# Top-k attention stage of a two-layer vision tower: when router weights and queries are loaded, and where the follow-up parts stand

## The reference

```python
# layer 1 attention: causal, but each query keeps only its 32 largest scores
scores = jnp.einsum('bhqd,bhkd->bhqk', q, k) / math.sqrt(D_HEAD)
scores = jnp.where(causal, neg_inf, scores)
vals, idx = jax.lax.top_k(scores, K_S)                  # K_S = 32
masked = jnp.put_along_axis(jnp.full_like(scores, -jnp.inf), idx, vals, axis=-1, inplace=False)
y = (softmax(masked) @ v) @ Wo.T + bo
h = h + y
# layer 1 router: a two-layer SELU network of 256 -> 1024 -> 256, and the two largest of its 256 outputs
gate_logits = selu(layernorm(h) @ gate_wi + gate_bi) @ gate_wo + gate_bo
topv, topi = jax.lax.top_k(gate_logits, 2)
```

## Time and profile before

| | |
|---|---|
| median of 3 runs | 2192.14 us (2188.59 to 2197.21) |
| the profiled execution's own time | 2191.06 us |
| its span | 2189.4 us |
| busy share of the span | DVE 67%, PE 66%, PEld 40%, ACT 38%, POOL 27% |
| `attend_top`, from its first DVE instruction to `weight` | 1198.0 to 2147.9 us |

### The profile page before, as it was taken

One profiled execution on the slowest core, in us unless ns is written; L12 is line 12 of the kernel. 1 busy time (PEld: TensorE's weight loads), 2 busy tenths in 40 slices (PEclk: granted clock), 3 DMA queues, 4 the chain that ended last, 5 costly groups with the idle time before them and its releaser, 6 DMA issues. The chain is left out here.

```text
span 2189.4 us, 35237 instructions
## 1 busy us (share of the span) xinstructions
PE 1453.4 (66%) x10364; PEld 865.4 (40%) x10397; DVE 1469.3 (67%) x4767; ACT 825.5 (38%) x2043; POOL 592.2 (27%) x1044
## 2 busy tenths in 40 slices
PE   6489888948887608999346266576656666666651
PEld 3122225524443504666223144454445444444440
DVE  4578876747775611111245499989997999799905
ACT  2256663215554202222013244355435443544320
POOL 4100001210000060000343144455435544554341
PEclk9699998969999758999758556567656665766675
DMA  5572220443331321111217400110021002100001
GB/s 162 162 261 66 77 66 8 137 133 78 77 77 70 169 77 36 46 43 44 68 49 207 111 1 1 40 40 1 1 47 32 2 1 50 30 2 1 1 1 39
DMA packets 87485, 137.61 MB, mean 63 GB/s; under 512 B 9720, under 2 KB 68000, under 8 KB 85540
## 3 DMA queue, kind: packets, MB, share of 16 engines
q1 hardware_dynamic: 84068, 127.38, 20.0%
q0 software_dynamic: 3264, 8.41, 1.2%
HBM read 82.50 MB, written 53.76 MB: 62 GB/s over the span
## 5 line engine op out<-in xcount | busy, mean ns | idle before, releaser
L1359 DVE MATCH_REPLACE8 top_left<-top_next,top_left 128x65 f32<-128x65 f32 (+15 forms) x768 | 322.2, 427 | 0.0
L1354 DVE MAX8 top_next<-top_left 128x8 f32<-128x65 f32 (+15 forms) x768 | 300.7, 432 | 0.0
L1255 POOL TENSOR_TENSOR top_e<-top_e,top_left 128x129 f32<-128x129 f32 (+15 forms) x256 | 191.3, 769 | 243.5 <-DVE top_left L1359 243.5
L1125 ACT ACTIVATE top_e<-top_ps_s,top_neg_max 128x129 f32<-128x129 f32 (+15 forms) x256 | 126.0, 492 | 344.3 <-POOL top_neg_max L1240 339.9
L1003 PE MATMUL top_ps_pt<-ident,top_e 128*128 128x128 f32 x640 | 149.7, 364 | 130.3 <-POOL top_e L1255 85.3
L686 DVE TENSOR_REDUCE tok_rowmax<-tok_ps_s 128x1 f32<-128x512 f32 x256 | 167.0, 688 | 42.4 <-PE tok_ps_s L528 39.7
L1901 DVE TENSOR_TENSOR moe_hid<-moe_act_gate,moe_ps_h 128x512 f32<-128x512 f32 x39 | 26.8, 688 | 220.0 <-ACT moe_act_gate L1862 220.0
L1003 PEld LDWEIGHTS top_ps_pt<-ident,top_e 128*128 128x128 f32 x640 | 106.1, 189 | 153.5 <-issue 149.0
L686 DVE TENSOR_REDUCE rot_rowmax<-rot_ps_s 128x1 f32<-128x128 f32 (+3 forms) x256 | 115.7, 488 | 47.1 <-PE rot_ps_s L531 43.1
L659 ACT ACTIVATE tok_et<-tok_ps_st 128x1024 f32<-128x1024 f32 x128 | 124.2, 1021 | 51.6 <-PE tok_ps_st L562 51.6
L1801 PE MATMUL moe_ps_h<-moe_w,moe_rows_t 128*128 x312 | 142.3, 599 | 0.2 <-issue 0.2
(11 more groups left out here) (332 smaller groups left out, 3118.0 us busy)
## 6 DMA issues: line engine op xcount, KB each, us to landing
moe_w<-in_moe_w SPq DMA_DIRECT2D x3, 4096.0 KB, 24.0
moe_xs<-zeros SPq DMA_DIRECT2D x1, 5120.0 KB, 20.6
last_xs<-zeros SPq DMA_DIRECT2D x1, 5120.0 KB, 33.6
moe_rows<-moe_xs SPq DMA_DIRECT2D x40, 128.0 KB
moe_ys<-moe_y SPq DMA_DIRECT2D x38, 128.0 KB, 1.7
v_rows<-tok_va SPq DMA_DIRECT2D x4, 1024.0 KB
tok_vs<-v_rows SPq DMA_DIRECT2D x16, 256.0 KB
v_rows<-rot_va SPq DMA_DIRECT2D x4, 1024.0 KB
```

Of the source, the lines that this page charges most:

```text
L1125: act.activation(e[:, U % KEPT, 0:keys(U)], row(U), ACT.Exp, bias=neg_max[:, U % 4:U % 4 + 1]).then_inc(e_ok, 1)
L1255: pool.tensor_tensor(e[:, U % KEPT, 0:w], e[:, U % KEPT, 0:w], left[:, U % 4, 0:w], ALU.subtract).then_inc(prob_ok, 1)
L1354: dve.max(next8[:, U % 2, step // 2, :], left[:, U % 4, 0:keys(U)]).then_inc(pick, 1)
L1359: ins = dve.match_replace(left[:, U % 4, 0:w], next8[:, U % 2, step // 2 - 1, :], left[:, U % 4, 0:w], 0.0)
```

## The change

- The six weight tensors get their buffers ahead of `norm` (`upper_weights`), and SP issues their DMAs in `norm`, right behind the three of `top_w`, `top_qkb` and `top_vb`. They count on one semaphore, `c.upper_in`. `gate_bi` is negated by POOL at the start of `attend_top`; the wait and the instruction on DVE are gone.
- From the second image on a group's queries and keys wait for the last scores of the group in the image before (`s_mm`), no longer for its last product; the values still wait for that product. The values of group g are issued behind the queries and keys of group g+1, in the first image too.
- Follow-up parts are placed by half rounds. `follow(k, 0)` stands ahead of the round's work on PE and ACT, and in mid-round on DVE, right behind `largest`; `follow(k, 1)` stands at the end. On POOL both stand at the end. A planner walks over the half rounds with an estimated start of each, 0.8 + 0.0083 x keys us for each unit, and an estimated duration of each part, and places the parts of the normed run (`denominators` to `normed_out`) and the routed run (`hidden` to `search`) of neighbouring steps where they fit. It also keeps who used `ps_x` last, and `bank_free` waits for that.
- The two buffers of `summed`, `x_t`, `hid` and `logits` become one each.
- In the last step T=16 `scale`, `add_residual`, the final line of `normalise`, both `join` and `add_bias` run on DVE (the square root stays on POOL), and the second half of `hidden` writes a bank of the scores, so that it need not wait for the first.

The diff, cut to what is spoken of:

```diff
-        def step_at(k, lag):
-            T, rest = divmod(k - START - lag, 8)
-            return T if rest == 0 and 0 <= T < STEPS else None
+        NORMED = (("denominators", DVE, 0.5), ("scale", POOL, 1.5), ("turn_context", PE, 2.0), ("context_out", ACTE, 1.0),
+                  ("project_out", PE, 4.0), ("sum_copy", ACTE, 1.0), ("residual", POOL, 2.0), ("moments", DVE, 1.0),
+                  ("normalise", POOL, 3.0), ("turn_normed", PE, 2.0), ("normed_out", ACTE, 1.0))
+        ROUTED = (("hidden_0", PE, 4.0), ("hidden_out_0", ACTE, 3.0), ("hidden_1", PE, 4.0), ("join_0", POOL, 0.0),
+                  ("hidden_out_1", ACTE, 3.0), ("join_1", POOL, 3.0), ("route", PE, 8.0), ("logits_out", ACTE, 1.0),
+                  ("add_bias", POOL, 1.0), ("search", DVE, 1.0))
+        begins, at = [], 0.0
+        for k in range(rounds):
+            own = sum(0.8 + 0.0083 * keys(U) for U in (2 * k, 2 * k + 1))
+            begins += [at, at + own / 2]
+            at += own
...
+        while routed_run[0] < STEPS:
+            for run, parts in ((routed_run, ROUTED), (normed_run, NORMED)):
+                ahead_of = -1
+                while run[0] < STEPS:
+                    T, i, free = run
+                    name, engine, us = parts[i]
+                    if free > (begins[half] if ahead_of < 0 else begins[half + 1] - us) or engine <= ahead_of:
+                        break
+                    if name in TO_BANK and in_bank:
+                        break
...
+                    step_of[name, half] = T
...
+                    ahead_of = engine if engine != DVE else 9
+                    run[:] = (T, i + 1) if i + 1 < len(parts) else (T + 1, 0), max(free, begins[half]) + us
...
         @block.sync
         def _(sp):
             for b in range(B):
-                for g in range(G):
-                    if b:
-                        sp.wait_ge(pv_mm, G * (NQ * b - 1) + g + 1)
-                    load_step(sp, c, b, g, qs[g], ks[g], loaded[g])
-                    load_by_position(sp, c, b, g, vs[g], v_loaded[g])
-                if b == 0:
-                    sp.dma_start(wo[:, :, :], a["top_wo"]).then_inc(w_in, 16)
...
+                for g in range(G + 1):
+                    if g < G:
+                        if b:
+                            sp.wait_ge(s_mm, PER_TILE * (NQ * b - 1) + 4 * g + 4)
+                        load_step(sp, c, b, g, qs[g], ks[g], loaded[g])
+                    if g:
+                        if b:
+                            sp.wait_ge(pv_mm, G * (NQ * b - 1) + g)
+                        load_by_position(sp, c, b, g - 1, vs[g - 1], v_loaded[g - 1])
...
@@ VectorE
                     if 2 * k + 3 < units:
                         largest(2 * k + 2)
                         largest(2 * k + 3)
+                follow(k, 0)
+                if k < rounds:
                     for step in (2, 4):
...
                     for u in pair:
                         take(u, 6)
-                follow(k)
-                if k == START:
-                    dve.wait_ge(w_in, 16 * 6)
-                    dve.tensor_scalar(less_bi[:, :], gate_bi[:, :], -1.0, None, ALU.mult).then_inc(ready, 1)
+                follow(k, 1)
...
-def norm(c, tag, fetch):
+def norm(c, tag, fetch, ahead):
...
             c.fetch(sp, fetch)
+            for dst, src in ahead:
+                sp.dma_start(dst, src).then_inc(c.upper_in, 16)
```

More of the change, by code:

```diff
@@ L810, in attend_top @@
     KEPT = 8
-    START = 2
     STEPS = NT + 1
+    LAST = STEPS - 1
+    READY = 3
+    PE, ACTE, POOL, DVE = range(4)
+    UPPER = 16 * 6
+    wo, bo = w_out
+    gate_wi, gate_bi, gate_wo, gate_bo = gate
     HC = HIDDEN // P
@@ new lines, in attend_top @@
+        ROUTED = (("hidden_0", PE, 4.0), ("hidden_out_0", ACTE, 3.0), ("hidden_1", PE, 4.0), ("join_0", POOL, 0.0),
+                  ("hidden_out_1", ACTE, 3.0), ("join_1", POOL, 3.0), ("route", PE, 8.0), ("logits_out", ACTE, 1.0),
+                  ("add_bias", POOL, 1.0), ("search", DVE, 1.0))
+        TO_BANK = ("turn_context", "project_out", "turn_normed", "hidden_0", "hidden_1", "route")
+        FROM_BANK = ("context_out", "sum_copy", "normed_out", "hidden_out_0", "hidden_out_1", "logits_out")
@@ new lines, in attend_top, with bank_free @@
+        LAST_ROUND = half // 2 + 1
+        def bank_free(eng, name, T):
+            if bank_before[name, T] is not None:
+                part, t = bank_before[name, T]
+                sem, count = {"context_out": (ct_out, t + 1), "sum_copy": (sum_out, t + 1),
+                              "normed_out": (x_out, t + 1), "hidden_out_0": (relu_ok, 2 * t + 1),
+                              "hidden_out_1": (relu_ok, 2 * t + 2), "logits_out": (l_out, t + 1)}[part]
+                eng.wait_ge(sem, count)
@@ L943, in tile, with due @@
+        def due(name, k, half):
+            return step_of.get((name, 2 * k + half))
         def tile(T):
@@ L1064, in hidden @@
                 r = rows(T)
+                out = hid_bank(T, half)
                 pe.wait_ge(x_out, T + 1)
[L1066 to L1071 removed]
+                if half and T == LAST:
+                    pe.wait_ge(e_ok, units)
+                else:
+                    bank_free(pe, ("hidden_0", "hidden_1")[half], T)
                 for i in range(HALF):
@@ L2463, in program @@
             w_top, get_top = projection_buffers(c, wide, a, "top")
-            norm(c, "mixed", get_top)
+            norm(c, "mixed", get_top, ahead)
             project(c, "top", *w_top, cls=True)
-        attend_top(c, "top", a, idx, weight)
+        attend_top(c, "top", w_out, gate, idx, weight)
+        upper.close()
         dispatch(c, "last", c.ctx, idx)
```

282 lines of the change are left out of this document (156 added, 126 removed).

## The result

The changed kernel takes 2137.49 us (median of 4 runs, 2135.94 to 2139.44), the kernel before 2190.36 us beside it (4 runs, 2186.03 to 2197.21). The ratio is 0.9759, with a 95% interval of 0.9746 to 0.9773: 53 us faster. Predicted were 2146 us and a range of 2120 to 2168. The profiled execution took 2137.56 us, with a span of 2135.8.

A forecast was written before the change was run, and what follows sets the result against it. DVE was taken to bound the rounds, so only its idle at start, boundaries and tail could be saved: 16.8 + 16 - 10.6 + 23.9 = 46.1 us. That gave 2145.0 us for the profiled execution, 2146 as median; range 2120 to 2168.

The forecast's parts named there:

- Start: Top stage's start: the 19.17 us wait for weights goes, late groups take some back; 16.8 us saved, bounds 12 to 21.
- the six issues cost nothing: In norm: SP has nothing else to do, so issuing the six weight tensors there was costed at nothing.
- The quarter of 8.6 us: At the start: moving values back brings groups 1 to 3 forward by up to 2.1 us; 1.7 taken.
- Boundaries: Three image boundaries: each costs DVE 7.5 instead of 12.8 us; 16 us saved, bounds 0 to 38.
- J=1: Rounds of 4.5 to 6 us at a boundary: waits of 3.6, 5.7 and 4.0 us fall to 1.5 each.
- J=0: Short 3 us rounds at an image boundary: waits for ACT, POOL and PE total 6 us, against 8.3 on average before.
- Mid-round waits: New DVE waits for POOL: moments four times 2.0 us, search twice 1.3; 10.6 us lost, bounds 5 to 16.
- Tail: From DVE's last top-k instruction to the last search's end: 42 us instead of 66; 23.9 saved, bounds 17 to 29.
- the placement works everywhere: Rival: all boundary waits go, mid-round waits are hidden; 79 us saved, 2113 us; 12% for it or near it (under 2132).
- it costs as much as it gives: Rival: boundaries give nothing, wider tiles gain extra waits; 6 us saved, 2186 us; 18% including half way.
- heads of rounds on PE hold the scores: Rival: PE parts heading rounds delay scores; with half lying open, 101 us over 16 steps, 2236 us; 4%.
- weights hold `q_parts`: Rival: weights land late in norm or project and delay q_parts; the start gives 0, 2163 us; 4%.

The follow-up runs named there:

- the run with the old loads: Changed kernel with queries, keys and values of a group issued together as before, from the second image on after the group's last product: 2139.73 us.
- the last experiment: Changed kernel with three edits: no VectorE part in its writer's half round, route kept out of half rounds under 2 us, step 15's route behind step 16's second hidden: 2111.08 us.
- the run with the old places: Changed kernel with follow-up parts back at the ends of the rounds where they stood before, all else as changed: 2168.69 us.
- step 15's route moved: Changed kernel with route, logits_out, add_bias and search of step 15 moved behind step 16's second hidden: 2131.39 us.

## Why the prediction was right, point by point

**The sum.** Predicted were 22.2 us from the rounds (16.8 + 16 - 10.6) and 23.9 from the tail; 27.0 and 25.3 came. By the waits, the rounds are 14.4 + 23.8 - 14.2 = 24.0; some 3 us more lie in no row of a wait: DVE is busy 1.2 us less between the two marks (803.0 against 804.3), and the rest, some 2 us, was not traced to a row. That the rounds came as near as 4.8 us is in part luck: the boundaries gave 7.8 us more than predicted, and start and mid-round waits together 6.0 less.

**Start, 16.8 predicted, 14.4 by the waits.** The step that was a little off is what comes late behind the weights. Group 1 came 1.05 us earlier, not 1.7, and the groups behind it left 2.50 and, with what follows group 3, 2.97 us, where I had 1.9 and 2.2; the wait for group 0 is 0.4 us longer. That the six issues cost nothing was right. The quarter of 8.6 us that I credited to moving the values was too much: the run with the old loads puts all of it under 1 us.

**Boundaries, 16 predicted, 23.8 came.** The mechanism was right: no DMA in it, the `route` of 6.50 us in a 3 us round stays, and ACT's first wait falls. The mis-sized term is J=1: I left 1.5 us each, and nothing was left but one gap of 0.30. J=0 was 4.8 us on average, predicted 6: ACT's first wait is 0.41, 0.83 and 0.58 and not 1.4, its second 0.94 and not 1.3, and the wait behind the route 3.99, 2.79 and 2.38, 3.05 on average and not 3.3.

**Mid-round waits, 10.6 predicted, 14.2 came.** `moments` of steps 3, 7, 11 and 15 wait 1.87 or 1.88 us (predicted 2.0), `search` of steps 1 and 2 wait 1.21 (1.3). Not foreseen were the searches of steps 4, 8 and 12, 1.35 each. They stand at the end of a round in the same half round as `logits_out`, and ACT's queue has a copy of the value product ahead of it, which waits for PE (ACT 1518.43, then 1518.60, then POOL 1519.06, in the timeline of the kernel after). I had looked for readers beside their writers in mid-round only. It is not the place alone: the searches of steps 5, 6, 9, 10, 13 and 14 stand beside their `logits_out` too, but in rounds of 417 to 513 keys and not of 289 and 321, and wait for nothing.

**Tail, 42.1 us predicted from the last top-k instruction, 40.7 came.** From the last MATCH_REPLACE8 to `denominators` it took 13.5 instead of 15.6 us, since the value product ended 1.1 us sooner than I had it and the way from `route` to `denominators` took 2.1 us and not 3.1; the normed run 7.6 instead of 7.5, the routed run 19.5 instead of 19.0. The one-input part of `join` is 0.43 us on DVE and not 0.7: I had put 512 elements at 0.7 us from the 410 ns for 256, and they take 426 ns.

**The rivals.** That the placement works everywhere (2113 us, or half of it 2130) did not come by the change, but the last experiment comes to that time: 2111. It does so by another sum, with 7.8 us left at the boundaries and a tail 5.1 us shorter than the change's. That it costs as much as it gives (2186) is refuted by the run with the old places: it is worth 31 us net. That heads of rounds on PE hold the scores shows in no row of a wide round, only behind `route` in the J=0 rounds; that weights hold `q_parts` shows in none.

## What to carry to other kernels

When a part is moved to an earlier place in an engine's queue, ask in which queue the writer of its input stands and what is ahead of it there; a planner needs this as a rule (no reader in the slot of its writer), since here each other rule that it got shuffled the pairs anew. Move a part with all that depends on it, and not alone: the four queues were laid out for each other, and a wait taken from one came back as a longer one in the others. And judge edits of one schedule together as well as apart: three that gave 11 us in sum gave 26 together.

## What the runs showed of the hardware

**VectorE and one input.** A one-input TENSOR_SCALAR on VectorE took 411 ns with 256 elements and a per-row scalar pair (L1027), and 426 ns with 512 elements and one constant (L1035); the two differ in form, so the length alone is not told apart. On GpSimd it was 1242 and 1497.

**VectorE behind GpSimd.** The same TENSOR_TENSOR of 512 elements that takes 0.69 us took 1.06 us twice, both times begun 0.2 us after an addition of GpSimd. Timeline of the kernel with all three edits:

```profile
2058.14 0.72 POOL L1063 TENSOR_TENSOR gate_logits<-gate_scaled,gate_bo 128x256 f32<-128x256 f32 x1 [12.84 <-ACT gate_scaled L1314]
2058.35 1.06 DVE L1055 TENSOR_TENSOR top_left<-gate_lifted,gate_high 128x512 f32<-128x512 f32 x1
```

It ended 0.55 us after the addition did. The Trainium skill (SBUF — State Buffer, section "SBUF: two separate sides") says that the two engines lock a shared pair of ports for a whole instruction when VectorE reads two inputs from SBUF and GpSimd reads SBUF. These two cases go that way, though an instruction of 0.69 us that began only when the lock was free would have ended 0.14 us later than it did; no other run was made on it.

**The clock in the tail.** The last `route`, 8 products of 128x256, took 5.62 us in the kernel after, 3.72 with step 15's route moved, and 5.41 with all three edits. Busy time and granted clock by stretch (columns as in the earlier trace rows), first around the last two routes of the kernel with the moved route, then of that with all edits:

```profile
2076.10:2079.80 3.70, 3.69 (x19) 2.92 (x17) 1.12 (x2) 2.35 (x9) 0.00 (x0) 1.00 0.00 0
2079.80:2082.80 3.00, 0.00 (x0) 0.00 (x0) 1.46 (x3) 1.67 (x6) 0.72 (x1) 1.00 0.00 0
2082.80:2086.60 3.80, 3.72 (x16) 2.96 (x16) 0.86 (x4) 0.00 (x0) 0.00 (x0) 1.00 0.00 0
```

```profile
2052.40:2056.10 3.70, 3.68 (x19) 2.92 (x17) 1.12 (x2) 2.35 (x9) 0.00 (x0) 1.00 0.00 0
2056.10:2059.40 3.30, 0.00 (x0) 0.00 (x0) 1.48 (x3) 1.96 (x7) 0.72 (x1) 1.00 0.00 0
2059.40:2062.20 2.80, 2.73 (x10) 2.31 (x11) 0.85 (x4) 0.00 (x0) 0.00 (x0) 0.77 0.00 0
2062.20:2064.90 2.70, 2.67 (x8) 1.82 (x6) 0.00 (x0) 0.00 (x0) 0.00 (x0) 0.61 0.00 0
```

After some 9 us of busy PE in both and a pause of 3.1 us in one and 3.4 in the other, the clock stayed at 1.00 (2.4 GHz) in the first execution and fell towards 0.50 (1.2 GHz) in the second, and the route cost 1.7 us more. So this term of a tail moved by 1.7 us with the same order of PE's work; whether the 0.3 us of pause set it or something else is left open, with one execution of each. It is also why the tail with all edits came to 35.5 us and not 33.7.
